# A decoder layer on one core: the output product of fourteen head pairs as seven block products

## The reference, cut to what matters

```python
qkv = silu(x @ qkv_w.T)                # per head q, k, v of 128
o = ((q @ k.T) * decay) @ v            # causal, decay per head (the scan over blocks, summed up)
o = norm_w * o * rsqrt(mean(o * o) + eps)   # mean over all 32 heads
o = sigmoid(x @ gate_w.T) * o
x = layernorm(x + o @ out_w.T)         # the output product: 4096 -> 1024
```

## Time and profile before

| | before |
|---|---|
| median of three runs | 1945.26 us |
| the profiled execution's own time | 1945.45 us |
| its span, first to last instruction | 1943.5 us |
| instructions | 25465 |
| TensorE (PE) busy | 1854.2 us, 95% |
| VectorE (DVE) busy | 1311.7 us, 67% |
| ScalarE (ACT) busy | 871.2 us, 45% |
| GpSimd (POOL) busy | 488.0 us, 25% |

### The profile page before, as it was taken

How to read it: one execution, slowest core, us unless ns; L and a number is a source line. 1 busy time by engine, 2 the same in 40 slices (tenths; PEclk the granted TensorE clock), 3 DMA queues, 4 the chain that set the end, 5 groups by cost and what they waited for, 6 DMA issues and landing times.

```text
span 1943.5 us, 25465 instructions
## 1 busy us (share of the span) xinstructions
PE 1854.2 (95%) x9361; PEld 888.4 (46%) x9361; DVE 1311.7 (67%) x1820; ACT 871.2 (45%) x1282; POOL 488.0 (25%) x400
## 2 busy tenths in 40 slices
PE   7999999999999999999999999999999999998885
PEld 5344444444444444444444444444444444564321
DVE  7676666767676766667675766666675757578856
ACT  5453444434453544434353534444343535434553
POOL 2232122222232122221232221222222321211433
PEclk9999999999999999999999999999999999998988
DMA  4112222231222222231321212222211212134321
GB/s 182 47 65 87 63 90 66 76 93 49 93 82 87 66 87 65 87 87 44 97 77 55 76 66 45 76 66 76 61 49 60 82 55 66 60 101 155 93 71 76
DMA packets 117787, 149.59 MB, mean 77 GB/s; under 512 B 67233, under 2 KB 83745, under 8 KB 117281
## 3 DMA queue, kind: packets, MB, share of 16 engines
q1 hardware_dynamic: 106208, 135.29, 22.5%
q0 software_dynamic: 2560, 8.39, 1.3%
q10 hardware_dynamic: 8896, 4.28, 0.8%
HBM read 119.63 MB, written 12.58 MB: 68 GB/s over the span
## 4 chain that ended last, share of the span: by engine, by line
PE 74%; DVE 9%; ACT 5%; DMA 5%; issue 4%; POOL 3%; ACTq 0%; POOLq 0%; DVEq 0%
PE bank L1114 18%; PE bank L1141 15%; PE bank L1143 15%; PE bank L1142 15%; DMA v_split<-w_vo 3%; ACT w_pair L1292 2%; DVE w_pair L1410 2%; DMA raw_pair<-w_vt 2%; PE bank L1183 2%; PE bank L1185 2%; PE bank L1184 2%; PE bank L1251 1%; PE bank L1259 1%; DVE bank L1465 1%; POOL raw_pair L1631 1%
## 5 line engine op out<-in xcount | busy, mean ns | idle before, releaser
L1141 PE MATMUL bank<-x_blocks,w_pair 128*128 128x512 f16 (+1 forms) x1820 | 679.4, 373 | 14.7 <-DVE bank L1453 7.3
L1142 PE MATMUL bank<-x_blocks,w_pair 128*128 128x512 f16 (+1 forms) x1820 | 678.9, 373 | 0.0
L1143 PE MATMUL bank<-x_blocks,w_pair 128*128 128x512 f16 (+1 forms) x1820 | 678.8, 373 | 0.0
L1114 PE MATMUL bank<-w_vo,gated_split 128*128 128x512 f16 x1440 | 331.9, 380 | 0.1
L1630 POOL TENSOR_TENSOR sums_pair<-raw_pair 128x512 f32<-128x512 f32 x63 | 88.3, 1402 | 854.3 <-DVE w_pair L1410 643.7
L1141 PEld LDWEIGHTS bank<-x_blocks,w_pair 128*128 128x128 f16 x1820 | 178.4, 98 | 218.7 <-DVE bank L1453 15.7
L1143 PEld LDWEIGHTS bank<-x_blocks,w_pair 128*128 128x128 f16 x1820 | 178.4, 98 | 203.7 <-issue 1.4
L1142 PEld LDWEIGHTS bank<-x_blocks,w_pair 128*128 128x128 f16 x1820 | 178.4, 98 | 192.5 <-issue 1.1
L1114 PEld LDWEIGHTS bank<-w_vo,gated_split 128*128 128x128 f16 x1440 | 141.1, 98 | 170.2 <-issue 1.9
L1410 DVE SCALAR_TENSOR_TENSOR w_pair<-raw_pair,w_pair 128x1024 f16<-128x1024 f32 x126 | 177.8, 1411 | 48.1 <-ACT w_pair L1292 48.1
L1639 POOL TENSOR_TENSOR ssq<-ssq,sig 128x512 f32<-128x512 f32 x64 | 82.6, 1291 | 447.5 <-ACT sig L1346 447.5
(11 more groups left out here) (182 smaller groups left out, 2105.9 us busy)
## 6 DMA issues: line engine op xcount, KB each, us to landing
raw_pair<-w_qk SPq DMA_DIRECT2D x32, 1024.0 KB, 5.0
raw_pair<-w_gate SPq DMA_DIRECT2D x16, 1024.0 KB, 4.8
raw_pair<-w_out SPq DMA_DIRECT2D x16, 1024.0 KB, 5.1
raw_pair<-w_vt SPq DMA_DIRECT2D x15, 1024.0 KB, 4.9
decay_sb<-decay SPq DMA_DIRECT2D x32, 256.0 KB, 5.2
raw_pair<-ctx_in SPq DMA_DIRECT2D x8, 1024.0 KB, 4.8
acc<-x_t SPq DMA_DIRECT2D x4, 1024.0 KB, 11.2
ctx<-raw_pair SPq DMA_DIRECT2D x8, 512.0 KB, 2.8
```

The lines of the kernel that those rows point to most:

```text
L1114: last = pe.matmul(out, a, b, start=m == 1, stop=m == n)
L1141: pe.matmul(out, w_hi, x_hi, start=unmet and k == 0, stop=False, skip_group_check=halves or not fresh)
L1142: pe.matmul(out, w_hi, x_lo, start=False, stop=False, skip_group_check=halves or not fresh)
L1143: mm = pe.matmul(out, w_lo, x_hi, start=False, stop=k == QT - 1, skip_group_check=halves or not fresh)
```

## The change

1. For pairs 0 to 13 the output product of a row tile (both sequences, both halves of columns) becomes seven block products in four stages (`out_stage`): products 1 and 7, then 2 and 6, then 5 and 4, then 3. A block is one (unit or sum of units) times one (block of weights or difference of blocks), three matmuls of 128x512. Three banks of the ring are taken by a row tile; bank 0 is copied into the second (ScalarE), and six additions go to the accumulator.
2. The gated unit is no longer written over its bank and split from there. It goes to float32 buffers in SBUF; GpSimd makes four sums of units (`sum_units`); seven blocks are split (`split_block`).
3. GpSimd makes four differences of the output weights (`wo_sum`); seven blocks of them are split in three parts (`split_wo`).
4. The works between the products are placed anew in every round from 1 to 14.
5. The buffers of weights and gated blocks grow, and the descriptor area of GpSimd's DMAs is set to 2048 bytes of a partition.

```diff
+G_BLOCK = {0: 0, 2: 1, 3: 2, 1: 3}
+S1, S2, S3, S4 = 3, 4, 5, 6
+OUT_PRODUCTS = {1: (0, 0, 0), 2: (1, 2, 0), 3: (S4, 3, 1), 4: (2, 6, 2), 5: (S1, 1, 1), 6: (S2, 5, 1), 7: (S3, 4, 2)}
+OUT_STAGES = ((1, 7), (2, 6), (5, 4), (3,))
+N_BLOCKED = NG - 2
...
+    def wo_sum(self):
+        item = self.unsplit[0]
+        t3, item["t1"], item["t2"], item["t4"] = (self.tick("pair_sum") for _ in range(4))
+        self.add("wo_sum", slot=item["slot"], landed=item["landed"], free=self.tmp_free, t1=item["t1"], t2=item["t2"])
+    def split_wo(self, part):
+        ready = (item["t1"], item["t1"], item["t4"])[part]
+        self.add("wo_split", part=part, slot=item["slot"], ready=ready, free=[self.vo_free] + self.v_turned[1:],
+                 hi=self.tick("w_hi"))
...
     def attend(self, n, unit):
-        self.aring.give(bank, self.g_done[(h % GH, b)])
+    def split_block(self, block, src, ready):
+        self.add("g_split", block=block, src=src, ready=ready, free=self.g_free[block], hi=self.tick("g_hi"))
+        self.g_done[block] = self.g_split = self.tick("g_lo")
+    def gated(self, n, unit):
+        done = self.gate_free[h % GH] = self.g_unit[unit] = self.tick("gated")
+        if not blocked:
+            done = self.split_block(G_BLOCK[unit], ("bank", bank), done)
+        self.aring.give(self.attended["i"], done)
+    def sum_units(self, block):
+        after = {S3: [self.g_unit[0], self.g_unit[1], self.g_done.get(0)], S2: [self.g_unit.get(3), self.g_done.get(S3)],
+                 S1: [self.g_unit.get(3), self.g_summed], S4: [self.g_done.get(1), self.g_summed]}[block]
+        self.add("g_sum", block=block, after=after)
+    def out_stage(self, n, s, stage):
+        before = {1: free[0], 7: free[2], 2: read.get("seed"), 6: read.get("seed"), 5: read.get("u2"), 4: read.get("p7"),
+                  3: read.get("u4")}
...
+        if stage == 0:
+            read["p7"] = add(2, 1, 1, mms[1])
+        elif stage == 1:
+            self.main_ring.give(at["ring"][0], add(0, 0, 0, mms[0]))
+            read["u2"] = add(1, 1, 0, mms[1])
+        elif stage == 2:
+            read["u4"] = add(1, 1, 1, mms[0])
+            self.main_ring.give(at["ring"][2], add(2, 1, 0, mms[1]))
+        else:
+            self.main_ring.give(at["ring"][1], add(1, 0, 1, mms[0]))
...
         product_pair(plan, "gate", n, {
-            "p1": ([score(0)] if n == 1 else []) + [part(0)],
-            "p7": [attend(0), score(1)],
-            "p2": [part(1)],
-            "p6": [attend(1), score(2), gate(0)],
-            "p5": [part(2)],
-            "p4": [attend(2), score(3)],
-            "p3": [gate(1), split_vo],
+            "p1": [part(0), part(1)],
+            "p7": ([score(0)] if n == 1 else []) + [attend(0), gated(0), score(1)],
+            "p2": units(0),
+            "p6": [part(2), attend(1), gated(1), gate(0), score(2), wo_sum],
+            "p5": [wo(0)],
+            "p4": sums(S3) + [wo(1), attend(2), gated(2), score(3), wo(2)],
+            "p3": [gate(1)] + split_sum(S3),
...
         product_pair(plan, "q", n, {
-            "p1": [attend(3)] + gate_rest,
-            "p2": [part(0)] + out(0, 1),
-            "p6": [part(1)],
-            "p7": out(2, 3),
-            "p5": out(4, 5),
-            "p4": [part(2)],
+            "p1": [attend(3), gated(3)] + units(2) + gate_rest,
+            "p2": sums(S1) + stages(0) + split_sum(S1) + units(3) + sums(S2, S4) + split_sum(S2) + [part(0)],
+            "p7": stages(1) + [part(1)] + split_sum(S4),
+            "p5": stages(2),
+            "p3": stages(3) + [part(2)],
...
         product_pair(plan, "k", n, {
-            "p1": out(6, 7) + ([stash] if stashing else []),
-            "p2": [part(0)],
-            "p6": out(8, 9) + [part(1)],
-            "p5": out(10, 11) + [part(2)],
+            "p1": stages(4) + stages(5) + ([stash] if stashing else []),
+            "p7": stages(6) + [part(0)],
+            "p2": stages(7),
+            "p6": [part(1), part(2)] + stages(8),
+            "p3": stages(9) + [part(0)],
...
             product_pair(plan, "v", n, {
-                "p1": out(12, 13),
-                "p2": [part(0)],
-                "p6": out(14, 15) + [part(1)],
-                "p5": [part(2)],
-                "p4": [lambda: plan.scores(n, UNITS[0])],
+            "p7": stages(10) + stages(11) + [part(1)] + stages(12) + stages(13) + [part(2)],
+            "p2": stages(14),
+            "p6": [lambda: plan.scores(n, UNITS[0])] + stages(15),
...
-        self.vo = sb("w_vo", [P, 2, 2 * D], F16)
+        self.wo = sb("w_vo", [P, 2, 7, BLK], F16)
-        self.g_hl = [sb(f"gated_split{b}", [P, GH, 2, S], F16) for b in range(B)]
+        self.g = sb("gated_split", [P, 7, 2, S], F16)
+        self.gated32 = sb("gated32", [P, S], F32)
+        self.g32 = {unit: k_flat[:, i * D:(i + 1) * D].bitcast(F32) for unit, i in ((1, 0), (2, 1), (3, 2))}
+        self.g32[0] = self.gated32[:, :]
...
+        elif kind == "g_sum":
+            dst, a, op, b_ = {S3: (0, 0, ALU.subtract, 1), S2: (0, 3, ALU.subtract, 0), S1: (1, 1, ALU.add, 3),
+                              S4: (2, 2, ALU.subtract, 0)}[st["block"]]
+            pool.tensor_tensor(c.g32[dst], c.g32[a], c.g32[b_], op).then_inc(sem["g_sum"])
...
-    nc = bacc.Bacc("TRN2", target_bir_lowering=False, num_devices=1)
+    nc = bacc.Bacc("TRN2", target_bir_lowering=False, num_devices=1, dynamic_dma_scratch_size=2048)
```

More of the change, by code:

```diff
@@ L377, in out @@
         self.main_ring.give(bank, self.acc_done[(b, s, half)])
-        self.g_free[b] = st["mm"]
+        for i in range(GH):
+            self.g_free[G_BLOCK[i * B + b]] = st["mm"]
         if n < NG - 1:
@@ L703, in attend, with gated, stages @@
             return lambda: plan.attend(n - 1, UNITS[i])
+        def gated(i):
+            return lambda: plan.gated(n - 1, UNITS[i])
+        def stages(*steps):
+            return [lambda step=step: plan.out_stage(n - 1, step // 4, step % 4) for step in steps]
         def out(*js):
@@ L715, in end_v, with units, sums, split_sum @@
             return lambda: plan.end_v(vs[b], half)
+        blocked = 0 < n <= N_BLOCKED
+        def units(i):
+            return [lambda: plan.split_unit(i)] if blocked else []
+        def sums(*blocks):
+            return [lambda b=b: plan.sum_units(b) for b in blocks] if blocked else []
+        def split_sum(block):
+            return [lambda: plan.split_sum(block)] if blocked else []
+        def wo(part):
+            return lambda: split_vo(part)
         product_pair(plan, "gate", n, {
@@ L789, in out, with attend @@
             plan.out(n, j // 8, j // 2 % 4, j % 2)
+    def attend(unit):
+        plan.attend(n, unit)
+        plan.gated(n, unit)
     def some(phase, steps):
@@ L989, in stash_of, with wo_blocks, g_source, vo_part @@
         return raw, raw.bitcast(BF16)[:, :, 0:D]
-    def vo_part(self, part, slot, late):
+    def wo_blocks(self, part, slot):
+        blocks = (slice(0, 2), slice(2, 4), slice(4, 7))[part]
+        src = self.sums_pair[:, :] if part == 2 else self.raw_pair[:, slot, blocks]
+        return src.rearrange("p c m -> p (c m)"), [self.wo[:, n, blocks].rearrange("p c m -> p (c m)") for n in range(2)]
+    def g_source(self, src):
+        return self.banks[src[1]][:, :] if src[0] == "bank" else self.g32[src[1]]
+    def vo_part(self, part, slot, late, out):
         src = self.raw_pair[:, slot, 2 * part:2 * part + 2].rearrange("p c m -> p (c m)")
@@ L994, in vo_part @@
             return src.rearrange("p (c s) -> p c s", c=4), [self.vo_late[n][:, 4 * part:4 * part + 4] for n in range(2)]
+        if out:
+            return src, [self.wo[:, n, 2 * part:2 * part + 2].rearrange("p c m -> p (c m)") for n in range(2)]
         return src, [self.vo[:, n, part * D:(part + 1) * D] for n in range(2)]
@@ L1192, in tensor_program @@
             three(pe, c.banks[st["bank"]][:, :],
-                  [((c.g_hl[b][:, i, 0, cols], c.g_hl[b][:, i, 1, cols]),
+                  [([c.g[:, G_BLOCK[i * B + b], n, cols] for n in range(2)],
                     c.out_weights(i, st["half"], st["n"] == NG - 1))
                    for i in range(GH)]).then_inc(sem["out_mm"])
+        elif kind == "out_stage":
+            cols = slice(st["s"] * P, (st["s"] + 1) * P)
+            for p in st["products"]:
+                block, w, place = OUT_PRODUCTS[p["i"]]
+                out, fresh, last = c.banks[st["banks"][place]][:, :], p["i"] in (1, 7), p["i"] in (2, 3, 4)
+                until(pe, sem, p["before"])
+                pe.wait_ge(sem["g_lo"], p["g"][1])
+                pe.wait_ge(sem["w_lo"], p["w"][1])
+                g_hi, g_lo = (c.g[:, block, n, cols] for n in range(2))
+                w_hi, w_lo = (c.wo[:, n, w] for n in range(2))
+                pe.matmul(out, g_hi, w_hi, start=fresh, stop=False, skip_group_check=not fresh)
+                pe.matmul(out, g_hi, w_lo, start=False, stop=False, skip_group_check=not fresh)
```

(5 more changed lines are left out.)

156 lines of the change are left out of this document (123 added, 33 removed).

## The result

The changed kernel takes 1957.76 us (median of 4 runs, 1956.59 to 1958.68) and the one before 1944.89 us (4 runs, 1941.65 to 1946.1). The ratio is 1.0068, 95% interval 1.0051 to 1.0086: 12.9 us slower, where 1944 was forecast, inside the stated range. The profiled execution has a span of 1956.8 us.

What follows compares the result with a forecast made beforehand. TensorE, busy for 95% of the span, was taken to set the time. Work of 1451.1 us plus waits of 59.5 and 1.6 gave 1512.2 us for the main part, against 1513.4, so 1944 us in all, range 1905 to 1964.

Steps and rivals of the forecast that it cites:

- Work: TensorE's matmul time per round: 84 output matmuls in place of 96, 2.59 us less, 103.65 us a round.
- First attention: Wait at each round's first attention product, with split and load now before product 2 of `v`: 0.15 us a round.
- Neighbouring stages: TensorE waits where output stages stand together: 0.2 us at stages 4 and 5, 0.3 and 0.3 at stages 10 to 13.
- the 0.2 us more in rounds with context: In `k`, `u3` late by 0.2 us in eight rounds, where GpSimd sums weights beside the split of `part(0)`.
- `q`, the point that decides: From the fourth attention to product 5 of `q`: TensorE waits for S2's split, then `u3`, 3.3 us a round.
- alternation: In `q`, VectorE splits with two SBUF inputs and GpSimd sums exclude each other and take turns, making `u3` late.
- the rivals' signs: 105 us rounds with 0.69 us splits; first-attention gaps over 1 us; final scatters over 2.5 us apart.
- the whole free case: Rival: sums and splits in `q` pass each other, 43 us less, 1902 us; chance 0.20.
- Descriptor area: Forecast value 0 for the 2048-byte area; rival, the last scatters go serially, 10 to 20 us, 1957; chance 0.06.
- The sum: Main part: 1451.1 us of work + 14 x (3.3 + 0.8 + 0.15) + 8 x 0.2 = 1512.2 us, against 1513.4.

Runs made afterwards that it cites:

- the earlier splits of `v` alone: Kernel before, with only the weight splits of `v` placed one product earlier: 1929.35 us, ratio 0.9913.
- the late sums: Changed kernel with GpSimd's four weight sums for `k` held until `u3` of `q` is done: 1948.28 us, ratio 1.0018.
- its wait filled: Changed kernel with nine, or five, useless matmuls a round into idle bank 7 ahead of product 5 of `q`: 1939.72 us, or 1938.08.
- the order alone: Changed kernel with only VectorE's order changed in `q`, S4's split ahead of `part(1)` and `part(1)` behind stage 2: 1965.17 us, ratio 1.0103.
- the runs with 4.16 and 4.44 us of waits a round: Changed kernel with GpSimd's sums for `k` held until `u3`, 1948.28 us; that plus VectorE's reordering in `q` and stages 5 to 15 spread, 1956.17 us.
- the single wait of 3.46 us: Kernel before with six more VectorE operations on bank 1 ahead of `u3` of `q` in rounds 1 to 14: 2014.82 us, ratio 1.0359.

## Why the prediction was wrong

Point by point.

*Work.* Predicted 103.65 us a round, measured 103.7. Right: 2.6 us less than before.

*First attention.* Predicted 0.15 us, measured none. Right; in the kernel before, the earlier splits of `v` alone do it (1929.35 us).

*Neighbouring stages.* Predicted 0.2 + 0.3 + 0.3 = 0.8 us, measured 0.19 + 0.30 + 0.30 = 0.79. Right, place by place. Only the 0.2 us more in rounds with context is not there.

*`q`, the point that decides.* Predicted 3.3 us by alternation, measured 0.76 + 2.12 = 2.9, with splits of 1.03, 1.75, 1.75 and 2.29 us and sums of 1.6 to 2.1, and none of the rivals' signs. Right in place and mechanism, 0.4 us too much in size. That the late sums remove it (splits of 0.68 us behind a first one of 1.03, which still meets the last sum of units, and a wait for `u3` of 0.36) shows it; that the whole free case was worth 43 us was not to be had from the sums alone, as the run of 1948.28 us shows.

*Descriptor area.* Value 0; the ratio of 1.0003 (0.9993 to 1.0013) tells no difference.

*The sum, the step that failed.* It priced the wait as time in which TensorE stands still: 14 x 4.25 + 1.6 = 61.1 us. The waits were indeed less, 51.5 us. What it had no term for is the time after the wait. The main part then stood at a granted clock of 1.00, and I took matmuls at 0.216 us for granted. Around the end of the two waits in `q` the clock falls to 0.50 for some 3.4 us, 21.4 us lost in 13 rounds, and 1.7 more at the first attention of round 1. With that term, the measured waits and the 0.5 us of small ones the sum is 1451.7 + 51.5 + 23.1 + 0.5 = 1526.8 us, as measured. Without it the kernel would take some 1935 us by the sum; with its wait filled it takes 1939.72 and 1938.08, under the kernel before: the sign of the change hung on this term. No rival named it either. That 1944 and 1957.76 us are only 14 us apart is partly luck: the waits were put 9.6 us too high, the clock 23.1 us too low. The rows could have warned. The longest wait of a quiet round before was 1.1 us between starts (0.93 us idle), so no row of that trace's main part showed what 2 us and more would do. But just ahead of the main part the same trace of the kernel before does: TensorE waits for 2.4 us, and 1.1 us behind the restart the clock is at 0.50.

```profile
81.19 0.38 PE L1141 MATMUL bank<-x_blocks,w_pair 128*128 128x512 f16 x1 [2.24 <-DVE w_pair L1410]
82.30:85.70 3.40, 3.40 (x10) 0.50 0.80 294
```

From these rows a term could have been put beside the wait of 3.3 us: 0 if the clock holds, and, as an estimate, 3.4 us at half speed, 1.7 us lost a round, if it falls.

Open: why the clock did not fall in the round at 1420, which has the same waits to 0.01 us, and from what wait on it falls. With 0.77 + 1.05 us it never did in `q`; with 0.76 + 2.12 us it did in 27 of 28 rounds (the kernel after and the one with the order alone), with 3.46 us in 12 of 14. The wait of 2.4 us at about 80 us stands in all twelve kernels, and the clock falls at it in seven of them and not in five. So the same wait can bring the fall or not, and its length alone doesn't tell. In the runs with 4.16 and 4.44 us of waits a round, none single over 1.3 us, it did not fall in `q`.

## What to carry to other kernels

A wait of TensorE can cost more than its length: read the granted clock and the starts behind it, and where it can't be removed, matmuls of no use in it can pay (18.0 us here). VectorE's splits with two SBUF inputs and GpSimd's sums took turns here, so hold GpSimd's batch back until VectorE's urgent chain is through, and then check what stands behind the held result in VectorE's own order. When a change comes with a new placement, time the placement alone: here it was worth 16 us, more than the seven products gave at their best.

## What the runs showed of the hardware

In the kernel after, half clock lasted about 3.4 us each time, and its start moved against the restart of TensorE behind the same waits: 0.6 us ahead of it in round 1, 0.15 ahead in round 2, then some 0.13 us later in each round, up to 1.3 us behind it in round 12; round 13 had none, and in round 14 it was 0.13 us ahead again. With the order mended alone it settled at 0.5 us ahead of the restart, still inside the wait, and cost 1.4 us instead of 1.7. After the single wait of 3.46 us it began between 1.2 us ahead of the restart and 0.3 us behind it; three times it lasted 6.8 us. With splits and sums side by side, a VectorE split of 128x512 took 1.75 us against 0.68, one of 128x1024 2.29 against 1.21, and a GpSimd sum 1.6 to 2.1 against 1.27. Their turns can be followed by the ends of records: each split of the four in front of `u3` ends 0.55 us (128x512) or 1.09 us (128x1024) behind the end of a sum, and each sum 1.12 us behind the end of a split.
